# A two-layer graph network: ScalarE's one-hots ahead of its weight copies, and ranks summed right behind a group's last count

## The chip, the cores and the metric

The kernel runs on one core of a Trainium2 chip. The time is device microseconds of one execution. Three runs of the kernel before gave 1287.24, 1288.93 and 1292.48 us; the median is 1288.93.

## The reference

50,000 nodes with 256 features `x`, 12,500 edges with `src`, `dst` and 128 edge features. Two layers, each added to its input and normalised over the row (mean, variance):

```python
# layer 0: attention over incoming edges
h = x @ Wn.T + bn
e = edge_attr @ We.T + be
a = leaky_relu(sum((h[src] + e) * attn, -1), 0.01)
a = exp(a - segment_max(a, dst)[dst])
a = a / (segment_sum(a, dst)[dst] + 1e-16)
x = layernorm(x + relu(segment_sum(h[src] * a, dst)))
# layer 1: mean over neighbours (edge_index = [src, dst])
mean = segment_sum(x[dst], src) / max(count(src), 1)
x = layernorm(x + x @ W1.T + b1 + mean @ W2.T + b2)
```

Most nodes have no edge; for them layer 0 is only a normalisation.

## The kernel before, in words

The kernel is written for five engines by hand; each has its own program, and semaphores order them. Nothing is scheduled by a planner: the order on an engine is the order of its code.

**Tiles and groups.** The edges are 98 tiles of 128, padded to T = 100 tiles; four tiles are a group (Q = 25 groups). The nodes are 98 groups of 512 rows.

**Sorting by counting.** Edges are sorted twice, by `dst` (`DST`) and then by `src` (`SRC`). A key has a low digit (256 values) and a high digit (196). For every edge a one-hot row of each digit is made in `X`: VectorE (DVE, `onehots`) makes all low ones and five of eight high ones, ScalarE (ACT, `high_onehots`) the other three of eight, each in two steps (|digit - i| into a spare tile, then Relu(1 - it)). TensorE (PE, `sort`) multiplies them, eight matmuls a group, into a histogram in bank 7 that counts the edges of every key. DVE (`starts`) turns it into start positions, which PE seeds into the table in bank 2. Then come the *lookups* (DVE `tiles`, PE in `sort`, ACT): two tiles at a time ACT copies the table, PE adds the two tiles' counts to it, and looks up the copy with one-hots of the low digit spread across partitions (`low_across` on DVE, `upper_across` on ACT, made from low digits that SP loads). DVE compares keys within a tile (`earlier`), picks the looked-up count with `found_rank` two tiles later, and for a group sums both into ranks (`ranks`). During the DST lookups it also computes a product with the edge features (`features`).

**What the ranks release.** GpSimd (POOL) scatters one tile at a time of (key, other key, feature product) to its rank in HBM (`scatter_order`, line 506), each scatter waiting for the ranks of its group; at most 8 are in flight. When all 100 DST scatters have landed, `load_order` brings the sorted rows back (`ordrow`). DVE takes them in `ordered_rows(DST)` ahead of group 1 of the SRC lookups, and makes indices in `ordered_columns` and `ordered_ends` ahead of groups 2 and 3. With these, POOL gathers 100 tiles of `x` rows into `X` (line 497), then issues 20 SRC scatters, then 100 scatter-adds of layer 0's results into the copy `z_scratch` (line 544).

**Behind that.** DVE computes a dot of each gathered row with `v_b` (100 products), the softmax over the sorted edges follows, then layer 0's sums on PE. Then all node groups pass (`dense`, PE bound by its code), then the edges sorted by `src` (`by_src`).

**SP's queue.** In this order SP issues the key and weight loads, four loads of edge features, the low digits and keys spread over partitions for four groups (lines 396 and 398), then part of the 125 copies of `x` to `z_scratch` (line 372, 400 KB each): 20, two for every second group of DVE's DST one-hots, and then one or two for each group, with the spreads of later groups (three ahead) and more features between them. A second burst of copies is released by DVE's SRC one-hots. All copies must have landed before POOL's first scatter-add.

**The weights.** PE transposes Wn, W1 and W2 into banks 0 to 2 and forms products with the attention vector in banks 3 to 5. ACT copies them out: three copies of 128x512 (line 651) and three shorter ones (653 to 655), counted by `s_wcp`. PE waits for `s_wcp` = 4 ahead of `sort(DST)`, because the sort uses banks 1 to 6; DVE waits for it behind its DST one-hots, since `features` needs `u_b`. There DVE also adds the identity to W1 (line 1212), so that the residual comes with the product. `centre_weights` (behind the SRC lookups) takes the mean out of W1's and W2's columns.

Of the kernel before, what the change touches and what calls it, by code (L numbers as in the profile page):

```python
# [5 lines left out]
P = 128  # L6
D = 256
DE = 128
# [8 lines left out]
ALU = mybir.AluOpType  # L17
# [6 lines left out]
DST, SRC = 0, 1  # L24
ORDER_AT = 1
FLIGHT = 8
HOOK = 48


def wait(eng, sem, value):  # L30
# [23 lines left out]
def build(nc, x, src, dst, edge_attr, Wn, bn, We, be, attn, W1, b1, W2, b2, out):  # L54
# [24 lines left out]
    with ExitStack() as ctx:  # L79
# [10 lines left out]
        bank = [ctx.enter_context(nc.psum_tensor(f"bank{i}", [P, 512], F32)) for i in range(8)]  # L90
# [9 lines left out]
        w1T = sb("w1T", [P, 2, D])  # L100
# [507 lines left out]
        def _(act):  # L608
# [37 lines left out]
                act.wait_ge(s_keyf, 2 * k + 2)  # L646
                act.dma_start(lowrow_dram[k], lowrow[k]).then_inc(s_keyd[k], 16)

            for w, t in enumerate((wnT, w1T, w2T)):
                act.wait_ge(s_wt, w + 1)  # L650
                a.copy(t[:].rearrange("p b c -> p (b c)"), bank[w][:, :]).then_inc(s_wcp, 1)
            act.wait_ge(s_vu, 1)
            a.copy(v_b, bank[3][:, 0:D])
            a.copy(u_b[:], bank[4][:, 0:DE])
            a.copy(c0[:], bank[5][:, 0:1]).then_inc(s_wcp, 1)

            gaps = [0]

# [10 lines left out]
            def high_onehots(k, q):  # L669
                n = k * Q + q  # L670
                wait(act, s_hotA, n - 1)
                at = [(GT * q + j, gap_hi[2 * (n % 2) + j // 2]) for j in range(GT) if high_by_act(GT * q + j)]
                made = [gap(o, iota16[:, 0:HC], -1.0, dig_f[k][:, 1, t:t + 1]) for t, o in at]
                for (t, o), m in zip(at, made):
                    ins = is_zero(onehot_hi[:, t, :], o, m)
                ins.then_inc(s_hotA, 1)
# [19 lines left out]
            for k in (DST, SRC):  # L696
                if k == SRC:
                    act.wait_ge(s_add[DST], T)
                for q in range(Q):
                    high_onehots(k, q)  # L700
                act.wait_ge(s_hotA, (k + 1) * Q)
                if k == DST:
                    act.wait_ge(s_zero, 80)
                upper_across(k, 0)
                act.wait_ge(s_seed, k + 1)
                for i in range(T // 2):
                    wait(act, s_add[k], 2 * i)
                    wait(act, s_look[k], 2 * (i - 1))
                    a.copy(table[i % 2].rearrange("p b c -> p (b c)"), bank[2][:, 0:2 * HC]).then_inc(s_tab, 1)  # L709
                    if i % 2 == 0 and i // 2 + 1 < Q:  # L710
                        upper_across(k, i // 2 + 1)
                    if k == SRC and i == 2 * ORDER_AT + 5:
                        store_sorted(DST)
# [86 lines left out]
        def _(dve):  # L800
# [54 lines left out]
            def features(t):  # L855
                if t > FT:
                    return
                c, i = (t // EC, t % EC) if t < NEC * EC else (NEC + t - NEC * EC, 0)
                if i == 0:
                    dve.wait_ge(s_ea[c % 4], 16 * (c // 4 + 1))  # L860
                feature_dot(xin[c % 4], i, t, P if t < FT else LT)
# [39 lines left out]
            def ranks(k, q):  # L901
                dve.wait_ge(s_found[k], GT * q + GT)
                s = slice(GT * q, GT * q + GT)
                v.tensor_tensor(rank_i[k][:, s], earlier[:, s], found[:, s], ALU.add).then_inc(s_rank, 1)

            def tiles(k, between):
                low_across(k, 0)
                for q in range(Q):
                    n = k * Q + q
                    if q in between:  # L910
                        between[q]()
                    dve.wait_ge(s_kb[n % 4], 16 * (n // 4 + 1))
                    keys = keyB[n % 4]
                    for j in range(GT):
                        t = q * GT + j
                        odd = j % 2
                        if 2 <= t < GT:
                            dve.wait_ge(s_lbT, n + 2)
                        else:
                            wait(dve, s_found[k], t - 3)  # L920
                        ins = stt(pair_junk[odd], keys[:, (j - odd) * P:(j + 1) * P], pay[:, t:t + 1, k],
                                  earlier_mask[:, 1 - odd:2, :].rearrange("p b c -> p (b c)"), ALU.is_equal, ALU.mult,
                                  accum_out=earlier[:, t:t + 1])
                        if j == GT - 1:
                            ins.then_inc(s_kbu, 1)
                        if t >= 2:
                            found_rank(k, t - 2)
                        if k == DST:
                            features(t)
                        if j == 1 and q + 1 < Q:  # L930
                            low_across(k, q + 1)
                    if q >= 1:
                        ranks(k, q - 1)
                found_rank(k, T - 2)
                found_rank(k, T - 1)
                ranks(k, Q - 1)
# [115 lines left out]

            def centre_weights():

                pair_stats(0, P, 0, w1T[:])
                pair_stats(0, P, 1, w2T[:])
                then(v.tensor_tensor(bias_rows[:, 0, :], bias_rows[:, 0, :], bias_rows[:, 1, :], ALU.add))
                then(pair_stats(1, P, 0, bias_rows[:, 0:2, :]))
                for i, w in enumerate((w1T, w2T)):
                    for b in range(2):  # L1060
                        ins = ts(w[:, b, :], w[:, b, :], stats[:, 0, 2 * i + b, 1:2], None, ALU.subtract)
                then(ts(bias_rows[:, 0, :], bias_rows[:, 0, :], stats[:, 1, 0, 1:2], None, ALU.subtract))
                ins = v.tensor_copy(bias_rows[:, 1, :], bias_rows[:, 0, :])
                ins.then_inc(s_wcen, 1)
# [142 lines left out]

            then(v.memset(pay[:, FT:T, 2], 0.0))
            onehots(DST)
            dve.wait_ge(s_wcp, 3)  # L1210
            for b in range(2):
                v.tensor_tensor(w1T[:, b, b * P:(b + 1) * P], w1T[:, b, b * P:(b + 1) * P], ident[:], ALU.add)
            dve.wait_ge(s_wcp, 4)
            starts(DST)
            tiles(DST, {})
# [119 lines left out]
        def _(pe):  # L1335
# [47 lines left out]
            def sort(k, after):  # L1383
                hist, tab = bank[7][:, 0:2 * HC], bank[2][:, 0:2 * HC]
                pe.wait_ge(s_onehot, k * Q + 1)
                nothing(hist, start=True, stop=False)
                for t in range(T):
                    if t % GT == 0:
                        pe.wait_ge(s_onehot, k * Q + t // GT + 1)
                        pe.wait_ge(s_hotA, k * Q + t // GT + 1)  # L1390
                    count_tile(hist, t)
                nothing(hist, start=False, stop=True).then_inc(s_hist, 1)

                pe.wait_ge(s_rowtot, k + 1)
                tot = scanned[:, :, HC - 1:HC].rearrange("p b c -> p (b c)")
                mm(bank[1][:, 0:2], above[:], tot, start=True, stop=False, skip_group_check=True)
                mm(bank[1][:, 1:2], ones[:], tot[:, 0:1], start=False, stop=True, skip_group_check=True).then_inc(s_offs, 1)
                pe.wait_ge(s_base, k + 1)
                mm(tab, ident[:], base.rearrange("p b c -> p (b c)"), start=True, stop=False,
                   skip_group_check=True).then_inc(s_seed, 1)  # L1400

                for q in range(Q):
                    n = k * Q + q
                    for i in range(GT * q // 2, GT * q // 2 + GT // 2):
                        pe.wait_ge(s_tab, k * T // 2 + i + 1)
                        for t in (2 * i, 2 * i + 1):
                            count_tile(tab, t).then_inc(s_add[k], 1)
                        if 2 * i == GT * q:
                            pe.wait_ge(s_lbT, n + 1)
                            pe.wait_ge(s_lbA, n + 1)  # L1410
                        for t in (2 * i, 2 * i + 1):
                            wait(pe, s_found[k], t - 3)
                            j = t % GT
                            for b in range(2):
                                ins = mm(bank[3 + t % 4][:, 0:HC], onehotT[n % 2][:, b, j * P:(j + 1) * P], table[i % 2][:, b, :],  # L1415
                                         start=b == 0, stop=b == 1)
                            ins.then_inc(s_look[k], 1)
                    if q in after:
                        after[q]()
                nothing(tab, start=False, stop=True)  # L1420
# [35 lines left out]
                wait(pe, s_y, GT * (h - 2) + 2 * p + 2)  # L1456
                products(rbank(par, p), [(turned_rows(xT[2 * par + p], parts(h)), w1T)], parts(h)).then_inc(s_r, 1)

            pe.wait_ge(s_wcp, 4)
            sort(DST, {})  # L1460
            sort(SRC, {ORDER_AT: lambda: turn_ordered(DST), ORDER_AT + 1: lambda: shift_ordered(DST)})

# [153 lines left out]
```

## Time and profile before

| | |
|---|---|
| median of three runs | 1288.93 us (1287.24 to 1292.48) |
| profiled execution, its own time | 1285.87 us |
| its span, first to last instruction | 1284.1 us |
| mean granted TensorE clock | 0.935 |
| busy: PE, DVE, ACT, POOL | 1069.7, 970.6, 646.1, 752.2 us |
| HBM traffic | 236 GB/s over the span |

The profile is of one execution. A row of the timeline gives the start and the length in us, the engine, the line of the code, the operation and its tiles as output<-input, how many were merged into the row (x162), and in brackets the time for which the engine had nothing to do before it, with what ended that time. PEld is the loading of matmul weights, SPq, ACTq and POOLq are DMA issues. Tile names are given without their numbers; `own_rows`, `xT`, `sel`, `csel`, `agg` and `yout` are buffers with many uses. A row with [x us <-DMA y] says that the engine waited for a transfer into or out of y. A row that begins with a stretch (66.00:100.00) gives its length, the busy time and the instructions of PE, PEld, DVE, ACT and POOL in it, the granted clock, the busy share of the 16 DMA engines and GB/s. A row of the waits gives the total, the number and the longest. The granted clock is in parts of 2.4 GHz; 0.50 is the lower level, 1.2 GHz.

The stages, from the timeline: loads and weights to 22 us, DST one-hots to 52, DST lookups to 161, SRC one-hots to 193, SRC lookups to 303, dots and softmax to 372, layer 0's sums to 575, the pass over all nodes to about 1040, the edges by `src` to the end.

### The profile page before, as it was taken

What the parts mean: (1) busy time and instruction counts of PE and PEld (TensorE: products, weight loads), DVE (VectorE), ACT (ScalarE), POOL (GpSimd) and SP (SyncE); (2) the same over time, 40 slices, a digit from 0 to 9 for tenths busy, and PEclk for the clock granted to TensorE, in tenths of its full rate; (3) what the DMA queues carried; (4) which work ended last, traced back from release to release, by engine and by line L of the source; (5) the groups of instructions that cost most, each with busy time, mean ns of one, the idle gap of its engine ahead of it and who ended that gap; (6) DMA issues with size and microseconds to landing.
All of it is one profiled execution on the core that took longest, in us unless ns stands there. A gap on an engine that the chain in (4) does not pass through costs nothing. (4 is left out here: it accounts for less than half of the span.)

```text
span 1284.1 us, 23311 instructions
## 1 busy us (share of the span) xinstructions
PE 1069.7 (83%) x6258; PEld 942.2 (73%) x6258; DVE 970.6 (76%) x3610; ACT 646.1 (50%) x1525; POOL 752.2 (59%) x731
## 2 busy tenths in 40 slices
PE   4788867995069888409999999899999899999992
PEld 3577756884069777308888888788888699999882
DVE  8699996889765433318999999999999877776650
ACT  4756583561024332206776776577776544444441
POOL 1077772777778888854444410366565457777773
PEclk9899998998579999759999999999999999999997
DMA  5999795887627777655776776699999533333321
GB/s 162 330 258 268 179 254 139 270 256 271 250 53 121 106 104 103 71 113 198 244 245 239 244 245 242 222 327 317 328 329 326 181 99 122 114 127 120 121 87 48
DMA packets 118884, 251.51 MB, mean 196 GB/s; under 512 B 23908, under 2 KB 63959, under 8 KB 118802
## 3 DMA queue, kind: packets, MB, share of 16 engines
q1 hardware_dynamic: 75738, 183.99, 44.3%
q0 software_dynamic: 40432, 64.66, 22.4%
q10 hardware_dynamic: 2632, 1.89, 0.5%
q8 instruction: 37, 0.61, 0.2%
q14 instruction: 45, 0.37, 0.1%
HBM read 172.88 MB, written 130.62 MB: 236 GB/s over the span
## 5 line engine op out<-in xcount | busy, mean ns | idle before, releaser
L1436 PE MATMUL bank<-w1T,xT 128*128 128x256 f32 x1972 | 462.5, 381 | 2.1 <-ACT yout L624 2.0
L1436 PEld LDWEIGHTS bank<-w1T,xT 128*128 128x128 f32 x1972 | 365.7, 190 | 51.7 <-ACT xT L615 2.6
L506 POOL DMA_INDIRECT order_scratch<-pay,rank_i x200 | 195.4, 977 | 201.2 <-DVE xin L811 91.0
L624 ACT ACTIVATE yout<-bank,rstd 128x256 f32<-128x256 f32 x493 | 207.6, 488 | 21.9 <-DVE rstd L1330 21.4
L1047 DVE BATCH_NORM_STATS2 stats<-xin 128x6 f32<-128x512 f32 x239 | 154.0, 685 | 57.9 <-DMA xin<-z_scratch 27.7
L1047 DVE BATCH_NORM_STATS2 stats<-bank 128x6 f32<-128x512 f32 x247 | 166.2, 682 | 41.5 <-PE bank L1436 41.5
L544 POOL DMA_INDIRECT z_scratch<-xin,idx_out x100 | 156.1, 1561 | 32.6 <-issue 29.3
L619 ACT ACTIVATE std<-stats,eps_c 128x4 f32<-128x4 f32 x273 | 80.3, 301 | 183.1 <-DVE stats L1047 182.9
L497 POOL DMA_INDIRECT X<-z_scratch,idx_dst x100 | 95.5, 955 | 129.0 <-DVE xin L811 89.6
L811 DVE TENSOR_SCALAR xin<-xin,low_mean,rstd 128x256 f32<-128x256 f32 x477 | 167.0, 413 | 0.9
L1415 PE MATMUL bank<-sel,agg 128*128 128x196 f32 x800 | 158.8, 342 | 4.5 <-DVE bank L814 4.5
L1427 PE MATMUL bank<-ident,xin 128*128 128x128 f32 (+1 forms) x952 | 127.8, 274 | 34.8 <-DVE xin L811 34.7
L615 ACT COPY xT<-bank 128x512 f32<-128x512 f32 x247 | 145.6, 590 | 15.6 <-PE bank L1427 9.8
L1427 PEld LDWEIGHTS bank<-ident,xin 128*128 128x128 f32 (+1 forms) x952 | 112.0, 142 | 46.4 <-issue 34.6
L1415 PEld LDWEIGHTS bank<-sel,agg 128*128 128x128 f32 x800 | 134.5, 196 | 6.9 <-DVE bank L814 6.2
L500 POOL DMA_INDIRECT out_rows<-yout,idx_out x100 | 100.0, 1000 | 62.8 <-issue 52.4
L1501 PE MATMUL bank<-sel,X 128*128 128x128 f32 x800 | 109.2, 288 | 23.0 <-ACT agg L723 20.6
L1501 PEld LDWEIGHTS bank<-sel,X 128*128 128x128 f32 x800 | 104.2, 202 | 29.4 <-ACT agg L723 21.6
L497 POOL DMA_INDIRECT X<-in_x,idx_src x100 | 99.0, 990 | 44.5 <-issue 18.0
L1366 PE MATMUL bank<-X 128*128 128x196 bf16 x800 | 96.2, 257 | 32.7 <-ACT sel L709 17.0
L814 DVE SCALAR_TENSOR_TENSOR xin<-bank,xdot,own_rows 128x256 f32<-128x256 f32 x100 | 42.1, 477 | 95.7 <-DMA z_scratch<-xin,idx_out 78.9
L1366 PEld LDWEIGHTS bank<-X 128*128 128x128 bf16 x800 | 67.4, 101 | 61.8 <-ACT sel L709 31.8
(250 smaller groups left out, 1405.5 us busy)
## 6 DMA issues: line engine op xcount, KB each, us to landing
z_scratch<-in_x SPq DMA_DIRECT2D x125, 400.0 KB
xin<-z_scratch SPq DMA_DIRECT2D x97, 512.0 KB, 4.6
out_rows<-yout SPq DMA_DIRECT2D x97, 512.0 KB, 3.0
kB<-sorted_scratch SPq DMA_DIRECT2D x50, 256.0 KB, 3.4
yout<-keys_scratch SPq DMA_DIRECT2D x50, 128.0 KB
xin<-in_edge_attr SPq DMA_DIRECT2D x12, 512.0 KB, 7.5
yout<-low_digits_scratch SPq DMA_DIRECT2D x50, 64.0 KB
order_scratch<-pay,rank_i POOLq DMA_INDIRECT x200
```

Source lines behind the costliest of these rows:

```text
L497: g.indirect_dma_start(out=dst_ap, out_offset=None, in_=table, in_offset=where).then_inc(s, 16)
L506: g.indirect_dma_start(out=order_dram[k], out_offset=bass.IndirectOffsetOnAxis(ap=rank_i[k][:, t:t + 1], axis=0), in_=pay[:, t, :], in_off ...
L544: g.indirect_dma_start(out=z_dram, out_offset=column(idx_out[DST], GT * q + j), in_=xin[q % 4][:, j, :], in_offset=None, compute_op=ALU.ad ...
L615: a.copy(xT[dst_i][:].rearrange("p a b c -> p (a b c)"), src_bank[:, :]).then_inc(copied, 1)
L624: a.activation(yout[hu][0:rows, j, :], bank_of(j // 2)[0:rows, (j % 2) * D:(j % 2 + 1) * D], ACT.Copy, scale=rstd[0:rows, slot, j:j + 1]). ...
L811: return v.tensor_scalar(o, i, s1, s2, o0, o1) if o1 is not None else v.tensor_scalar(o, i, s1, s2, o0)
L1047: return v.bn_stats(stats[0:rows, slot, 2 * p:2 * p + 2, :].rearrange("p j s -> p (j s)"), pair.rearrange("p j c -> p c j"))
L1366: ins = mm(o[:, b * HC:(b + 1) * HC], onehot_lo[:, t, b * P:(b + 1) * P], onehot_hi[:, t, :], start=False, stop=False, skip_group_check=True)
L1415: ins = mm(bank[3 + t % 4][:, 0:HC], onehotT[n % 2][:, b, j * P:(j + 1) * P], table[i % 2][:, b, :], start=b == 0, stop=b == 1)
L1427: ins = tr(o[:, at:at + n], pair[0:n, jj, c * P:(c + 1) * P], ident[0:n, 0:n])
L1436: ins = mm(to, left, w, start=i == 0, stop=i == len(pieces) - 1)
L1501: ins = mm(bank[b][:, j * P:(j + 1) * P], X[:, GT * q + j, c * P:(c + 1) * P], sel[q % 2][:, j, :], start=True, stop=True)
```

## The change

It has four edits:

1. On ACT the weight copies move into a function that is called ahead of group 10 (`WEIGHTS_AT`) of the DST high one-hots; ten groups of one-hots now come first.
2. PE's wait for the weight copies moves from ahead of the DST histogram to behind it, ahead of the first matmul that writes bank 1.
3. DVE adds the identity to W1 in `centre_weights`, with a wait for the result, instead of between its DST one-hots and the start positions.
4. In the lookups DVE sums the ranks of group q-1 behind the second tile of group q, right after the last count of group q-1, instead of behind the fourth. This holds for both sorts.

```diff
+WEIGHTS_AT = 10
...
-            for w, t in enumerate((wnT, w1T, w2T)):
-                act.wait_ge(s_wt, w + 1)
-                a.copy(t[:].rearrange("p b c -> p (b c)"), bank[w][:, :]).then_inc(s_wcp, 1)
-            act.wait_ge(s_vu, 1)
-            a.copy(v_b, bank[3][:, 0:D])
-            a.copy(u_b[:], bank[4][:, 0:DE])
-            a.copy(c0[:], bank[5][:, 0:1]).then_inc(s_wcp, 1)
+            def copy_weights():
+                for w, t in enumerate((wnT, w1T, w2T)):
+                    act.wait_ge(s_wt, w + 1)
+                    a.copy(t[:].rearrange("p b c -> p (b c)"), bank[w][:, :]).then_inc(s_wcp, 1)
+                act.wait_ge(s_vu, 1)
+                a.copy(v_b, bank[3][:, 0:D])
+                a.copy(u_b[:], bank[4][:, 0:DE])
+                a.copy(c0[:], bank[5][:, 0:1]).then_inc(s_wcp, 1)
...
                 for q in range(Q):
+                    if k == DST and q == WEIGHTS_AT:
+                        copy_weights()
                     high_onehots(k, q)
...
                         if k == DST:
                             features(t)
+                        if j == 1 and q >= 1:
+                            ranks(k, q - 1)
                         if j == 1 and q + 1 < Q:
                             low_across(k, q + 1)
-                    if q >= 1:
-                        ranks(k, q - 1)
...
             def centre_weights():
 
+                for b in range(2):
+                    ins = v.tensor_tensor(w1T[:, b, b * P:(b + 1) * P], w1T[:, b, b * P:(b + 1) * P], ident[:], ALU.add)
+                then(ins)
                 pair_stats(0, P, 0, w1T[:])
...
             onehots(DST)
-            dve.wait_ge(s_wcp, 3)
-            for b in range(2):
-                v.tensor_tensor(w1T[:, b, b * P:(b + 1) * P], w1T[:, b, b * P:(b + 1) * P], ident[:], ALU.add)
             dve.wait_ge(s_wcp, 4)
             starts(DST)
...
                 pe.wait_ge(s_rowtot, k + 1)
+                pe.wait_ge(s_wcp, 4)
...
-            pe.wait_ge(s_wcp, 4)
             sort(DST, {})
```

On ACT, behind the last DMA of the key rows, this stood before (own_rows<-iota is the first step of a one-hot, X<-own_rows the second):

```order
L651 ACT_TABLE_LOAD
L651 COPY own_rows<-bank 128x512
L651 COPY w1T<-bank 128x512
L651 COPY w2T<-bank 128x512
L653 COPY own_rows<-bank 128x256
L654 COPY u_b<-bank 128x128
L655 COPY c<-bank 128x1
L662 ACTIVATE own_rows<-iota,own_rows 128x196 x2
L667 ACTIVATE X<-own_rows,ones 128x196 x2
```

Now the table load is followed by ten groups of one-hots, of which the ninth and tenth stand here, and only then by the copies:

```order
L664 ACTIVATE own_rows<-iota,own_rows 128x196 x2
L669 ACTIVATE X<-own_rows,ones 128x196 x2
L664 ACTIVATE own_rows<-iota,own_rows 128x196
L669 ACTIVATE X<-own_rows,ones 128x196
L653 COPY own_rows<-bank 128x512
L653 COPY w1T<-bank 128x512
L653 COPY w2T<-bank 128x512
L655 COPY own_rows<-bank 128x256
L656 COPY u_b<-bank 128x128
L657 COPY c<-bank 128x1
```

The copies moved behind the tenth group; nothing on ACT was added or dropped.

On DVE, in group 1 of the DST lookups (bank,found is `found_rank`, xin,pay is `features`, xT,earlier the comparison within a tile, agg<-yout is `low_across` for the next group), this stood before, from the second tile's count to the end of the group:

```order
L814 SCALAR_TENSOR_TENSOR bank6,found<-own_rows2,own_rows5,bank6 128x196
L814 SCALAR_TENSOR_TENSOR xin0,pay<-xin0,u_b 128x128
L811 TENSOR_SCALAR agg0<-yout2,slot_f 128x512
L814 SCALAR_TENSOR_TENSOR xT0,earlier<-yout1,pay,own_rows2 128x128
L814 SCALAR_TENSOR_TENSOR bank3,found<-own_rows2,own_rows5,bank3 128x196
L814 SCALAR_TENSOR_TENSOR xin0,pay<-xin0,u_b 128x128
L814 SCALAR_TENSOR_TENSOR xT0,earlier<-yout1,pay,own_rows2 128x256
L814 SCALAR_TENSOR_TENSOR bank4,found<-own_rows2,own_rows5,bank4 128x196
L814 SCALAR_TENSOR_TENSOR xin0,pay<-xin0,u_b 128x128
L904 TENSOR_TENSOR rank_i0<-earlier,found 128x4
```

and this stands now:

```order
L818 SCALAR_TENSOR_TENSOR bank6,found<-own_rows2,own_rows5,bank6 128x196
L818 SCALAR_TENSOR_TENSOR xin0,pay<-xin0,u_b 128x128
L908 TENSOR_TENSOR rank_i0<-earlier,found 128x4
L815 TENSOR_SCALAR agg0<-yout2,slot_f 128x512
L818 SCALAR_TENSOR_TENSOR xT0,earlier<-yout1,pay,own_rows2 128x128
L818 SCALAR_TENSOR_TENSOR bank3,found<-own_rows2,own_rows5,bank3 128x196
```

The ranks moved ahead of the low one-hot and of two tiles' work. One feature product lies between the count into bank 6, the last that these ranks need, and the ranks.

## Rows read from the trace of the kernel before

**Rows 1.** Page, part 1: busy us, share of the span, instructions.
```profile
PE 1069.7 (83%) x6258; PEld 942.2 (73%) x6258; DVE 970.6 (76%) x3610; ACT 646.1 (50%) x1525; POOL 752.2 (59%) x731
```

**Rows 2.** Timeline from 11 to 52 us: ACT, DVE and PE at the one-hots.
```profile
11.27 1.28 ACT L651 ACT_TABLE_LOAD   x1 [11.27 <-issue]
...
12.32 30.82 DVE L811 TENSOR_SCALAR X<-iota,own_rows 128x256 bf16<-128x256 bf16 x162
...
19.68 0.59 ACT L651 COPY w2T<-bank 128x512 f32<-128x512 f32 x1 [0.27 <-PE bank L1348]
...
22.20 0.83 ACT L662 ACTIVATE own_rows<-iota,own_rows 128x196 bf16<-128x196 bf16 x2
...
23.86 6.14 PE L1366 MATMUL bank<-X 128*128 128x196 bf16 x48 [1.14 <-ACT X L667]
...
49.73 0.79 ACT L667 ACTIVATE X<-own_rows,ones 128x196 bf16<-128x196 bf16 x2
...
51.77 1.01 DVE L876 TENSOR_TENSOR_SCAN csel<-own_rows,bank 128x196 f32<-128x196 bf16 x2 [8.22 <-PE bank L1362]
```

**Rows 3.** Timeline from 63 to 66 us: the first ranks.
```profile
63.38 0.48 DVE L811 TENSOR_SCALAR agg<-yout,slot_f 128x512 f32<-128x512 uint8 x1
...
65.56 0.16 DVE L904 TENSOR_TENSOR rank_i<-earlier,found 128x4 int32<-128x4 f32 x1
...
66.02 1.16 POOL L506 DMA_INDIRECT order_scratch<-pay,rank_i  x1 [60.31 <-DVE rank_i L904]
```

**Rows 4.** Timeline from 195 to 220 us: the last DST scatter to the first gather.
```profile
195.27 0.96 POOL L506 DMA_INDIRECT order_scratch<-pay,rank_i  x1 [0.30 <-issue]
...
204.93 0.62 POOL L517 DMA_DIRECT2D ordrow<-order_scratch  x1 [8.70 <-DMA order_scratch<-pay,rank_i]
...
207.70 0.24 DVE L940 COPY krow<-ordrow 100x128 f32<-100x128 f32 x1 [6.56 <-DMA ordrow<-order_scratch]
...
219.86 1.02 POOL L497 DMA_INDIRECT X<-in_x,idx_src  x1 [14.31 <-DVE idx_out L967]
```

**Rows 5.** Last gather, first scatter-add; waits of 200 to 380 us; one stretch.
```profile
348.15 0.95 POOL L497 DMA_INDIRECT X<-in_x,idx_src  x1 [0.30 <-issue]
...
377.44 1.64 POOL L544 DMA_INDIRECT z_scratch<-xin,idx_out  x1 [2.47 <-ACT xin L734]
...
DVE xT L814 <- DMA X<-in_x,idx_src: 6.7, 9, 0.9
...
340.00:360.00 20.00, 1.78 (x9) 0.91 (x9) 10.68 (x51) 0.00 (x0) 15.12 (x17) 0.50 0.20 56
```

**Rows 6.** SP's queue, waits for its loads, and the stretch of the DST lookups.
```profile
30.84 17.51 SPq L372 DMA_DIRECT2D z_scratch<-in_x  x26
...
54.85 0.33 SPq L396 DMA_DIRECT2D yout<-low_digits_scratch  x1
...
96.19 0.72 ACT L662 ACTIVATE own_rows<-yout,slot_f 128x512 bf16<-128x512 uint8 x1 [2.13 <-DMA yout<-low_digits_scratch]
...
99.33 0.43 DVE L814 SCALAR_TENSOR_TENSOR bank<-own_rows,bank 128x196 f32<-128x196 f32 x1 [0.33 <-PE bank L1415]
...
66.00:100.00 34.00, 28.83 (x198) 25.83 (x197) 33.67 (x213) 18.42 (x32) 25.28 (x26) 1.00 1.03 268
```

**Rows 7.** PE's lookups around DVE's wait, and the granted clock in that stretch.
```profile
208.97 2.98 PE L1415 MATMUL bank<-sel,agg 128*128 128x196 f32 x8 [3.82 <-DVE bank L814]
...
215.48 1.52 PE L1415 MATMUL bank<-sel,agg 128*128 128x196 f32 x8
...
208.00:214.00 6.00, 5.03 (x18) 4.88 (x19) 5.09 (x32) 1.82 (x3) 0.00 (x0) 0.50 0.21 47
```

**Rows 8.** Timeline: two dependent DVE steps; DVE in the SRC lookups.
```profile
218.14 0.26 DVE L960 TENSOR_TENSOR xdot<-keyc,prevk 128x100 f32<-128x100 f32 x1
218.44 0.26 DVE L961 TENSOR_TENSOR idx_tmp<-idx_tmp,xdot 128x100 f32<-128x100 f32 x1
...
298.43 0.43 DVE L814 SCALAR_TENSOR_TENSOR bank<-own_rows,bank 128x196 f32<-128x196 f32 x1 [0.58 <-PE bank L1415]
```

## The prediction

> **What bounds the kernel now.** I read the page first, then the timeline from the start, then POOL's own timeline. GpSimd (POOL) is busy for 59% of the span [rows 1], yet from 66 to 575 us it is the engine that the others follow: 100 order scatters, 100 gathers, 20 scatters, 100 scatter-adds, nearly without a pause. So the question is when POOL may start, and what holds it between its blocks.
>
> Its start hangs on the first histogram. VectorE (DVE) makes its one-hots from 12.32 to 43.14, while ScalarE (ACT) loads its table at 11.27, waits for the weight transposes, copies the weights and begins its one-hots at 22.20; its last ends at 50.52, and DVE gets the histogram at 51.77 after 8.22 us without work [rows 2]. The first ranks are written at 65.56 and POOL starts at 66.02, after 60.31 us of idling [rows 3].
>
> Next, POOL's first block ends: the last DST scatter is issued at 195.27, POOL waits 8.70 us for it to land, loads the order rows at 204.93, and DVE, which had reached that point of the SRC lookups, takes them at 207.70 after waiting 6.56 us. From them come the indices with which the gathers start at 219.86, POOL having idled 14.31 us [rows 4]. DVE reached the wait at 207.70 - 6.56 = 201.14. These two arrivals, POOL's chain and DVE's, decide the gain.
>
> What follows is released by that work. The last gather is issued at 348.15; DVE's last dots wait for gathers, 6.7 us in 9 waits; the scatter-adds begin at 377.44 [rows 5]. A shift of 219.86 should reach the end whole. The background copy of x, which must be done before 377.44, has DMA engines only 0.20 busy from 340 to 360 [rows 5], so it has about 17 us to spare.
>
> **The change, part by part.**
>
> *ACT's one-hots first.* Table load ends at 11.27 + 1.28 = 12.55, and digits and iota exist by then (DVE's start at 12.32 uses them). ACT's 25 groups took 50.52 - 22.20 = 28.32 us, 1.133 a group [rows 2]. Ten groups end at 12.55 + 11.33 = 23.9. The six copies: three are 0.59 us each [rows 2] and three shorter, so between 1.8 and 3.5 us; I take 2.3, nearer the low end because the short ones are half the size or less. ACT resumes at 26.2 and its last 15 groups end at 43.2, level with DVE's 43.14. With the lag seen before (50.52 to 51.77, 1.25 us) DVE gets the histogram at 44.4 instead of 51.77: **7.3 us earlier** (between 6.1 and 7.4 by the copies). TensorE (PE) must keep up: 200 counting matmuls at the 128 ns of its first batch, 48 in 6.14 us [rows 2], would take 25.6 us; from 22.2 that ends at 47.8 and leaves 4.0 us. But that batch worked off a backlog; I take the one-hots as the end and keep 4.0 as the low bound.
>
> *Ranks two tiles earlier.* In the DST lookups the sum moves from 65.56 to where DVE now starts the next low one-hot, 63.38: **2.2 us earlier** [rows 3]. POOL needs no other thing at that moment, so it starts 7.3 + 2.2 = 9.5 us earlier, at 56.5. Its pace, (195.27 - 66.02) / 99 = 1.31 us a scatter, 5.2 a group, is its own; ranks come faster than that. The last scatter is issued at 185.8, lands at 195.4 with the same wait, and the order rows are with DVE at 198.2.
>
> *What of the 7.3 us DVE's lookups keep.* Little, by this trace. SP queues 26 copies of 400 KB from 30.84 on for 17.51 us, released by one-hots that DVE makes at the same times as before. The loads of low digits and keys for the lookups stand behind them on the same queue, the first issued at 54.85, and from 66 to 100 the DMA engines are fully busy. At group 10 ACT still waits 2.13 us for its low digits (96.19), and DVE, through PE, 0.33 us (99.33) [rows 6]. So at that point the lookups have no lead over the loads. Starting them earlier does not start the copies earlier; these loads land when the copies and feature loads ahead of them are through. Bounds: nothing kept (DVE at 201.1 again) and all kept (193.8). I take 0.5, by the row at 99.33, which is the point of the stage that binds.
>
> That sets the order rows (198.2) before DVE (200.6): DVE no longer waits, and it is DVE's own arrival that ends last. Gain: 207.70 - 200.6 = 7.1 us. Late next is PE: while DVE waited, PE had run two lookup pairs ahead, which now lie on the path (its pair takes 1.52 us at the full clock, 215.48). Against this, PE idled 3.82 us before 208.97 and then had its granted clock at 0.50 (the level of 1.2 GHz) from 208 to 214, with 2.98 us for such a pair; without that idle time it should stay at the upper level and save 1.5 us there and 1 us in the next [rows 7]. I set the two against each other: zero, with 1 us either way.
>
> *Small edits.* The identity is added to w1T in the node-weight centring instead of in the 8.22 us gap: two 128x128 adds, under 1 us with a wait, covered by DVE's 6.7 us of waiting for gathers [rows 5]; without that cover up to 1 us. PE's wait for the weight copies moves behind the histogram, when they are 15 us old: nothing. In the SRC lookups the ranks now follow their last count directly. A waited DVE step there costs little: of two dependent steps, 0.26 us long, the second starts 0.30 us after the first, and DVE idles 0.58 us a group waiting for PE [rows 8]. In the DST lookups, where DVE has no idle time, a feature product (two DVE steps) lies between count and ranks, longer than the 0.04 us that the waiting step loses in that row. Both nothing; without product and idle time the row would give 24 x 0.04 = 1.0 us on DVE's arrival, and a sum of 6.1.
>
> The Trainium skill (VectorE: DVE Perf Modes, "The DRAIN you can't avoid") says that a semaphore between two DVE operations costs nothing extra, as the pipeline is emptied between them in any case. By that rule even the bare wait would be free and the sum would stay at 7.1; the 0.04 us in rows 8 are nearly that.
>
> **Sum.** 7.1 us. The profiled execution took 1285.87 us and would take 1278.8; it is 3.1 us below the median, 1288.93, from which I forecast **1281.8 us**. Some 0.5% (6.4 us) is what a measurement here tells from no change, so the forecast is just past it.
>
> **Rivals.**
> - *The lookups keep all 7.3 us* (loads overtake, or the queue had slack). DVE is at its wait at 193.8, the order rows come at 198.2 and decide: 9.5 us, 1279.4. For it: DVE is at work for 33.67 of the 34 us from 66 to 100 [rows 6], so the stage looks like DVE's. Against: the wait at group 10. Chance 0.20.
> - *The last scatter lands early as well.* POOL's landing wait of 8.70 us [rows 4] would have to be its neighbours' doing, and gone. If it fell by 4 us, the order rows came at 194.2, and with all of the shift kept the gain would be 13.5 us, 1275.4. The Trainium skill (DMA: Bandwidth & Descriptors, "Queues, rings and completion order") says that each DMA engine takes turns between the queues that have work, by which POOL's few bytes would not wait behind SP's copies. The 8.70 us were measured with such copies in flight, so the trace does not bear it out. Chance 0.03.
> - *The landing does not move.* The second burst of SP's copies runs beside the last scatters; if their landing goes by the end of that burst, which moves only with DVE, the order rows come at 203 to 206 and the gain is 2 to 5 us, say 1285.4. Against it stands only that the wait begins with POOL's own last issue. Chance 0.15.
> - *Slower: the moved ranks stall DVE in the DST lookups.* DVE has no idle time there [rows 6]. If the new wait cost 0.4 us in each of 24 groups, DVE would reach its wait at 201.1 + 9.6 = 210.7, 3 us later than now: 1291.9. It decides from (207.70 - 201.14) / 24 = 0.27 us a group. The row of 0.30 us between dependent steps speaks against it, and the feature product in between. Chance 0.05.
> - *The forecast*, DVE's arrival sets the gain, 5.5 to 8 us: 0.57. That ACT does start early is plain from its order; that the histogram then waits for PE instead is inside it, since 4.0 + 2.2 = 6.2 us on POOL's chain still gives 6.2.
>
> **How the numbers follow.** Faster by over 0.5%: the two early cases (0.23) and some three fifths of the forecast, whose lower part lies inside 0.5%: 0.57. Slower by over 0.5%: 0.04, the stall with its upper price. The rest, 0.39, within 0.5%. The range runs from 9.5 us of gain with 2 us for the scatter of medians (the runs shown span 5 us) to a gain of 3.5 with the same: 1277.4 to 1287.4.
>
> **What will show it.** After: ACT's first one-hot at 12.6; DVE's idle time before the scan from 8.22 to about 1 us; POOL's first scatter at 56 to 57; ACT waits for low digits in groups four to ten longer than before (the queue takes the shift back) and DVE's SRC one-hots starting at nearly the old time; no wait before the order rows; gathers starting 7 us earlier, and the same 7 us at 377 and at the end. The prediction is wrong if DVE's SRC one-hots start 4 us or more earlier (then more is gained), or if the order rows still make DVE wait with its arrival unmoved (then less).

## The result, and the profile after

The change made the kernel slower. Over 20 runs of each on one chip the changed kernel took 1294.68 us (1289.37 to 1297.25) and the kernel before 1289.33 us (1285.85 to 1294.62): ratio 1.0036, 95% interval 1.0025 to 1.0048, or 5.35 us more. The forecast was 1281.8 us with a range up to 1287.4: wrong in sign, and the median lies outside. The profiled execution has a span of 1291.9 us, against 1284.1 us before; single executions differ by a few us, so stages are compared between the two traces, and times between medians.

The timeline of the changed kernel, all engines, in order of time (start, duration, engine, line, what, and in brackets the idle time before it and what ended it):

```profile
13.15 0.81 ACT L664 ACTIVATE own_rows<-iota,own_rows 128x196 bf16<-128x196 bf16 x2
...
31.91 18.26 SPq L373 DMA_DIRECT2D z_scratch<-in_x  x26
44.95 1.01 DVE L880 TENSOR_TENSOR_SCAN csel<-own_rows,bank 128x196 f32<-128x196 bf16 x2 [1.18 <-PE bank L1366]
50.27 0.94 SPq L397 DMA_DIRECT2D yout<-low_digits_scratch  x1
55.28 0.15 DVE L908 TENSOR_TENSOR rank_i<-earlier,found 128x4 int32<-128x4 f32 x1
55.74 1.16 POOL L507 DMA_INDIRECT order_scratch<-pay,rank_i  x1 [50.03 <-DVE rank_i L908]
59.15 12.99 SPq L373 DMA_DIRECT2D z_scratch<-in_x  x2
63.38 0.15 DVE L908 TENSOR_TENSOR rank_i<-earlier,found 128x4 int32<-128x4 f32 x1
71.93 0.96 POOL L507 DMA_INDIRECT order_scratch<-pay,rank_i  x1 [0.66 <-issue]
76.09 0.72 ACT L664 ACTIVATE own_rows<-yout,slot_f 128x512 bf16<-128x512 uint8 x1 [14.82 <-DMA yout<-low_digits_scratch]
76.09 0.49 DVE L815 TENSOR_SCALAR agg<-yout,slot_f 128x512 f32<-128x512 uint8 x1 [12.56 <-DMA yout<-low_digits_scratch]
82.09 0.16 DVE L908 TENSOR_TENSOR rank_i<-earlier,found 128x4 int32<-128x4 f32 x1
82.53 0.96 POOL L507 DMA_INDIRECT order_scratch<-pay,rank_i  x1 [9.64 <-DVE rank_i L908]
...
198.90 1.05 POOL L507 DMA_INDIRECT order_scratch<-pay,rank_i  x1 [0.30 <-issue]
210.86 0.62 POOL L518 DMA_DIRECT2D ordrow<-order_scratch  x1 [10.92 <-PE bank L1370]
216.62 0.24 DVE L944 COPY krow<-ordrow 100x128 f32<-100x128 f32 x1 [6.32 <-DMA ordrow<-order_scratch]
228.65 1.02 POOL L498 DMA_INDIRECT X<-in_x,idx_src  x1 [17.18 <-DVE idx_out L971]
387.06 1.63 POOL L545 DMA_INDIRECT z_scratch<-xin,idx_out  x1 [2.33 <-ACT xin L738]
```

Up to 55.74 all went as meant. ACT's one-hots start at 13.15, the histogram is with DVE at 44.95 (51.77 in [rows 2]), the first ranks at 55.28 and POOL's first scatter at 55.74 (65.56 and 66.02 in [rows 3]): 10.3 us earlier. Then comes a wait that the kernel before did not have: until 76.09 DVE (from 63.5) and ACT (from 61.3) stand still for the low digits of group 4, whose load SP had issued at 50.27, 4.6 us *earlier* than before [rows 6]. POOL, which had scattered the ranks of three groups, runs out of ranks for 9.64 us. Its last scatter is issued at 198.90, 3.6 us later than in [rows 4], and the first gather at 228.65, 8.8 us later. (Ahead of the order rows `load_order` waits for nothing but the landing of the scatters; where the brackets name PE there, here and below, the profile guessed wrongly.)

What the DMA engines did in that time is seen in the stretches (busy us and count by engine, then granted clock, DMA share, GB/s). First the kernel before, then the changed one:

```profile
core 0: us, PE busy (x) PEld busy (x) DVE busy (x) ACT busy (x) POOL busy (x), PEclk, DMA share, GB/s
56.00:62.00 6.00, 5.42 (x24) 5.02 (x24) 2.77 (x16) 2.69 (x5) 0.00 (x0) 0.56 1.00 311
62.00:66.00 4.00, 3.70 (x26) 3.33 (x26) 4.00 (x27) 2.30 (x4) 0.00 (x0) 1.00 0.95 312
66.00:70.00 4.00, 3.70 (x27) 3.30 (x26) 4.00 (x25) 2.30 (x4) 3.07 (x3) 1.00 0.67 222
```

```profile
56.00:62.00 6.00, 5.40 (x38) 4.89 (x38) 6.00 (x41) 3.11 (x6) 4.78 (x5) 1.00 1.04 326
62.00:66.00 4.00, 1.79 (x13) 1.49 (x11) 1.53 (x11) 0.00 (x0) 3.09 (x4) 1.00 1.11 131
66.00:70.00 4.00, 0.00 (x0) 0.00 (x0) 0.00 (x0) 0.00 (x0) 2.15 (x3) 0.56 0.92 227
70.00:76.00 6.00, 0.00 (x0) 0.00 (x0) 0.00 (x0) 0.00 (x0) 1.93 (x3) 0.50 1.10 185
```

In the kernel before, the engines moved some 310 GB/s until 66 us and POOL had nothing in flight. In the changed kernel POOL issues scatters from 55.74 on. Their first packets show on the DMA engines between 60 and 62 us, when the rate is still 354 GB/s; from 62 to 66 the engines, busy throughout, move 131 GB/s. PE falls idle as well, and its granted clock drops to 0.50, the level of 1.2 GHz.

### The profile page after: what moved, and what is told of

Read it like the earlier page. It is cut to its first block and busy times, and to the rows that moved or that the text cites. A ratio compares the mean times of both kernels' runs of the same rounds, so it can differ in the third digit from the quotient of the medians.

```text
span 1291.9 us, 23312 instructions
## 1 busy us (share of the span) xinstructions
PE 1063.7 (82%) x6258; PEld 942.7 (73%) x6258; DVE 973.2 (75%) x3610; ACT 645.0 (50%) x1525; POOL 757.6 (59%) x731
## 5 line engine op out<-in xcount | busy, mean ns | idle before, releaser
L507 POOL DMA_INDIRECT order_scratch<-pay,rank_i x200 | 199.1, 995 | 200.6 <-DVE xin L815 90.5
L1370 PE MATMUL bank<-X 128*128 128x196 bf16 x800 | 92.4, 252 | 45.6 <-ACT sel L713 33.0
```

The lines of the kernel that those rows point to most:

```text
L507: g.indirect_dma_start(out=order_dram[k], out_offset=bass.IndirectOffsetOnAxis(ap=rank_i[k][:, t:t + 1], axis=0), in_=pay[:, t, :], in_off ...
L1370: ins = mm(o[:, b * HC:(b + 1) * HC], onehot_lo[:, t, b * P:(b + 1) * P], onehot_hi[:, t, :], start=False, stop=False, skip_group_check=True)
```

## The experiments

**Theory T**: the order scatters (POOL's), now earlier, run beside SP's burst of 26 copies and slow it, so that the loads behind the burst land late. **Rival O**: queue order alone; the load stands behind the copies and lands when it lands, and earlier lookups only wait longer. **Rival M**: the moved ranks hold up DVE or PE. **Rival C** (later): the placing of SP's copies is all that matters. All runs were timed in five rounds against the kernel before on the same chip; that kernel's median was 1286.76 us in the first four, 1286.85 in the next four, 1285.81 in the last. Expectations were written on the base of 1289; ratios are what can be compared.

**1. The scatters held back until group 4's low digits are there.** `s_lb[0]` reaches 32 with the second load into the first buffer, that of group 4.

```diff
+            pool.wait_ge(s_lb[0], 32)
             for t in range(T):
                 pool.wait_ge(s_rank, t // GT + 1)
```

> The changed kernel, with one wait more: POOL issues no order scatter of DST until the low digits of group 4 have landed. Theory T (scatters slow the burst): the copies on SP's queue lose their rate only because POOL's 12-byte scatters, now issued from 55.7 us, run beside them. With the scatters held back the burst drains at some 310 to 330 GB/s as in the kernel before, the low digits of group 4 land at about 66 to 69 us, and DVE's wait before group 4 falls from 12.6 to some 3 to 5 us; the lookups then end 7 to 9 us earlier than in the changed kernel, and the time is 1284 to 1288 us, if POOL catches up by the end of the lookups. Rival O (queue order alone: the load stands behind the copies and lands when it lands): the wait stays near 12 us and the time at 1294. Rival M (the moved ranks hold up DVE or PE): nothing changes, 1294 us.

Measured: 1293.9 us, ratio 1.0056 (1.0043 to 1.0069). The timeline:

```profile
31.37 17.14 SPq L373 DMA_DIRECT2D z_scratch<-in_x  x26
...
69.93 0.48 DVE L816 TENSOR_SCALAR agg<-yout,slot_f 128x512 f32<-128x512 uint8 x1 [6.96 <-DMA yout<-low_digits_scratch]
70.20 1.24 POOL L507 DMA_INDIRECT order_scratch<-pay,rank_i  x1 [64.48 <-DMA yout<-low_digits_scratch]
75.92 0.16 DVE L909 TENSOR_TENSOR rank_i<-earlier,found 128x4 int32<-128x4 f32 x1
193.10 1.01 DVE L881 TENSOR_TENSOR_SCAN csel<-own_rows,bank 128x196 f32<-128x196 bf16 x2 [1.11 <-PE bank L1367]
202.40 0.96 POOL L507 DMA_INDIRECT order_scratch<-pay,rank_i  x1 [0.30 <-issue]
```

And the DMA view of both kernels from 62 to 66 us (queue q1 carries SP's copies and loads, q0 POOL's scatters; packets, MB, time as a share of 16 engines). Changed kernel:

```profile
DMA packets 173, 0.52 MB, mean 131 GB/s; under 512 B 71, under 2 KB 71, under 8 KB 173
q1 hardware_dynamic: 123, 0.52, 108.6%
q0 software_dynamic: 50, 0.00, 2.3%
```

Scatters held back:

```profile
DMA packets 315, 1.24 MB, mean 311 GB/s; under 512 B 52, under 2 KB 75, under 8 KB 315
q1 hardware_dynamic: 315, 1.24, 100.8%
```

The stretch and the order of the queue are the same and only the scatters are gone: 311 GB/s instead of 131. A packet of SP's queue took on average 4 us x 16 x 1.008 / 315 = 0.20 us without scatters, and 4 x 16 x 1.086 / 123 = 0.57 us with them (a sum above 100% means that packets overlap), while the 50 packets of the scatters took 2.3% themselves. This is the worst stretch, not a constant: from 62 us until the load is there the means are 182 GB/s with scatters (to 76) and 277 without (to 70), and run 2 below, with scatters but a shorter burst, moves 335 GB/s from 62 to 66. DVE's wait fell from 12.56 to 6.96 us (T had expected 3 to 5) and the load was there at 69.93 instead of 76.09 (0.5 us of that because the burst began earlier). So both T and O hold a part: about 5.6 us of the wait is the scatters' doing and 7.0 us plain queue order. DVE's SRC scan is back at 193.10, where the kernel before had it (193.21). That the time did not fall, against T's figure, is POOL's: it did not catch up. It issued a scatter every (202.40 - 70.20) / 99 = 1.34 us and issued the last at 202.40, 7.1 us after the kernel before [rows 4].

**2. Ten copies less ahead of group 4**

```diff
             for i in range(10):
                 sp.wait_ge(s_onehot, 2 * i + 1)
-                copy_x(2)
+                copy_x(1)
```

> The changed kernel, with one copy of x instead of two at each of the ten steps of SP's early burst (16 copies instead of 26 ahead of the loads of group 4; the ten left over go out at the end of the sort with the others). Theory T and rival O both say that the loads of group 4 then stand behind 10 copies less, worth about 10 x 400 KB at 320 GB/s = 12.5 us: they land by about 57 us, before the lookups of group 4 need them (63.5 us), and the wait of 12.6 us goes. What is left of the 6.8 us by which the first lookups start earlier is kept: some 1278 to 1283 us, unless the ten copies cost their time again beside the gathers. Rival M (moved ranks): the stall stays and so does 1294 us.

Measured: 1281.44 us, ratio 0.9951 (0.9938 to 0.9964), 5.3 us faster than the kernel before. DVE no longer waits at group 4, and with ranks at their moved place: rival M, as written for DVE and PE, is out. Where it gains and what it gives back:

```profile
190.98 0.96 POOL L507 DMA_INDIRECT order_scratch<-pay,rank_i  x1 [0.30 <-issue]
195.36 0.62 POOL L518 DMA_DIRECT2D ordrow<-order_scratch  x1 [3.42 <-PE bank L1370]
210.99 1.02 POOL L498 DMA_INDIRECT X<-in_x,idx_src  x1 [15.01 <-DVE idx_out L971]
293.01 31.86 SPq L373 DMA_DIRECT2D z_scratch<-in_x  x33
373.67 1.64 POOL L545 DMA_INDIRECT z_scratch<-xin,idx_out  x1 [5.40 <-ACT xin L738]
```

The first gather is 8.9 us earlier than in [rows 4], the first scatter-add only 3.8 us earlier than in [rows 5]. 33 copies instead of 23 now go out beside the gathers, and POOL waits 5.40 us instead of 2.47 for ACT's rows before the first scatter-add. Run 5 below shows that the one causes the other: it is the kernel before with only these ten copies moved there, and it waits 6.13 us, with 161.1 instead of 157.6 us from first gather to first scatter-add. Run 7, with 23 copies there, waits 2.48.

**3. and 4. Each part alone.** Run 3 is the changed kernel with `ranks(k, q - 1)` put back behind the group's last tile; run 4 the kernel before with only the ranks moved.

> The changed kernel with the ranks put back to where they were, after the group's last tile. First ranks some 2.2 us later than in the changed kernel, so POOL's first scatter at about 58 instead of 55.7 us. Theory T: the scatters still start well inside the burst, the stall before group 4 is shorter by at most 2 or 3 us: 1291 to 1294 us. Rival M (the moved ranks are to blame): the stall goes, 1280 to 1283 us. Rival O: as the changed kernel, 1294.

> The kernel before with the ranks alone moved ahead of the group's last two tiles; ScalarE's one-hots stay behind the weight copies. POOL's first scatter at about 63.8 instead of 66.0 us, when the burst (over at about 66 to 68 us) is nearly drained. Theory T: a loss of 0 to 3 us against a gain of up to 2 us at the end of the DST lookups: 1287 to 1291 us. Rival M: slower by most of the 5 us that the change cost, 1293 to 1295 us. Rival O: no change or 2 us faster.

Measured: one-hots alone 1289.15 us, ratio 1.0016 (1.0000 to 1.0032), with 9.5 us of waiting at group 4; ranks alone 1288.41 us, ratio 1.0012 (1.0002 to 1.0022), with no such wait on DVE. Neither part is worth anything in this queue, and together they cost more than either (1.0036). The stall fits T: POOL starts at 65.25 (ranks alone, in a trace whose histogram came 2.9 us later than in [rows 2]), 59.02 (one-hots alone) or 55.74 us (both), the earlier, the more of the burst its scatters meet, and DVE waits at group 4 not at all, 9.52 and 12.56 us. M wanted the stall gone in run 3. T's figure of 2 to 5 us lost there was just about met, with 2. The times of runs 3 and 4 are not T's alone, though: the moved ranks have a price of their own on POOL, which is read behind run 8.

**5. to 8. Room in the queue.** Run 5 is the kernel before with the edit of run 2, its control. Run 6 takes the burst out of the changed kernel altogether. Run 7 moves ten copies of it ahead of SP's wait for the weights, so that they fill a time when the kernel before moved 5 GB/s (16 to 20 us) and 34 (20 to 24); it moves 394 and 345 there:

```diff
+            copy_x(10)
             sp.wait_ge(s_wt, 3)
             sp.wait_ge(s_vu, 1)
...
             for i in range(10):
                 sp.wait_ge(s_onehot, 2 * i + 1)
-                copy_x(2)
+                copy_x(1)
```

Run 8 is run 2 with the ranks at their old place.

> The kernel before with SP's early burst cut from 26 to 16 copies as in the run with ten copies less: the control for that run. Theory T: in the kernel before nothing waited for these loads, so nothing is gained in the DST lookups; the ten copies that go out later, beside the gathers of x, may cost up to the 5 us that the stretch from first gather to first scatter-add grew by there (157.6 us before, 162.7 with ten copies less): 1287 to 1292 us. Rival C (the shorter burst by itself made that run fast, whatever ScalarE does): 1281 to 1283 us.

> The changed kernel with the burst taken out: 6 copies instead of 26 ahead of the loads of group 4, 20 more at the end of the sort. Theory T: with 16 copies nothing waited any more at group 4, so the DST lookups gain at most 1 or 2 us more; the stretch of the gathers takes the second ten copies as well and grows by up to another 5 us: 1281 to 1287 us. If copies beside the gathers cost nothing: 1279 to 1281 us.

> The changed kernel with ten copies issued right behind the weight loads, where the queues moved 5 GB/s from 16 to 20 us and 34 from 20 to 24 us, and ten instead of twenty in the burst: 26 copies ahead of group 4 as in the changed kernel, and as many at the end. Theory T: the burst is drained some 8 to 10 us earlier, the low digits of group 4 land at about 60 to 64 us, DVE's wait there falls from 12.6 to 0 to 2 us, the first gather starts at 211 to 213 us and the gathers keep their 158 us: 1277 to 1281 us. Rival (the early copies hold up the keys, the low digits or the features that the first lookups need): the DVE scan is late by several us and the time is 1284 to 1290 us.

> The run with ten copies less, with the ranks put back to where they were before. Theory T: once the queue is clear, POOL's 100 scatters of DST at 1.31 us each start when the first ranks are there, so ranks 2.2 us later make the last landing, the order rows and the gathers 2 us later: 1282 to 1284 us against 1280 to 1282. Rival M (the moved ranks cost time on DVE): faster than that run, 1278 to 1280 us. If neither: the same.

| run | median us | ratio to before (95%) |
|---|---|---|
| 5: before, ten copies less | 1287.86 | 1.0010 (0.9997 to 1.0022) |
| 6: changed, burst out | 1280.44 | 0.9949 (0.9933 to 0.9965) |
| 7: changed, ten copies at the start | 1279.07 | 0.9937 (0.9919 to 0.9955) |
| 8: run 2 with old ranks | 1280.47 | 0.9952 (0.9936 to 0.9969) |

Run 5: the shorter burst alone gains nothing in the end (2.0 us at the first gather, given back by the ten copies beside the gathers), so C is out. Run 6 is no better than run 2: once nothing waits at group 4, still less in the queue is worth nothing. Run 7 is the fastest. Its timeline:

```profile
7.95 6.92 SPq L370 DMA_DIRECT2D z_scratch<-in_x  x10
35.33 10.10 SPq L370 DMA_DIRECT2D z_scratch<-in_x  x16
...
55.75 1.16 POOL L508 DMA_INDIRECT order_scratch<-pay,rank_i  x1 [50.03 <-DVE rank_i L909]
189.71 0.96 POOL L508 DMA_INDIRECT order_scratch<-pay,rank_i  x1 [0.30 <-DMA order_scratch<-pay,rank_i]
194.28 0.62 POOL L519 DMA_DIRECT2D ordrow<-order_scratch  x1 [3.61 <-PE bank L1371]
210.19 1.02 POOL L499 DMA_INDIRECT X<-in_x,idx_src  x1 [15.29 <-DVE idx_out L972]
369.47 1.63 POOL L546 DMA_INDIRECT z_scratch<-xin,idx_out  x1 [2.48 <-ACT xin L739]
```

POOL starts at the same moment as in the changed kernel (55.75), with as many copies ahead of group 4, and nothing waits there; the first gather is 9.7 us earlier than in [rows 4] and the first scatter-add 8.0 us earlier than in [rows 5]. The time is 7.8 us below that kernel's. Run 8 was the run on the ranks alone: T expected some 2 us slower than run 2, M faster, and it came out the same (0.9952 against 0.9951). Its order rows are loaded at 197.04, 1.7 us later than in run 2, but that does not show in the time.

Runs 2 and 8 differ in the ranks' place alone, and POOL tells them apart. In run 8 it starts 1.2 us later (58.49 against 57.31) and yet issues its last scatter 2.6 us *earlier* (188.37 against 190.98). A scatter itself takes POOL longer where the ranks are moved. All 100 DST scatters of five kernels (count: shortest, median and longest in ns, first and last start), in the order before, run 8, run 4, run 2, changed:

```profile
L506 POOL DMA_INDIRECT order_scratch<-pay,rank_i x100: 954/959/1218, 66.0 to 195.3; - x100
L507 POOL DMA_INDIRECT order_scratch<-pay,rank_i x100: 954/959/1162, 58.5 to 188.4; - x100
L506 POOL DMA_INDIRECT order_scratch<-pay,rank_i x100: 955/1008/1202, 65.2 to 198.9; - x100
L507 POOL DMA_INDIRECT order_scratch<-pay,rank_i x100: 955/1010/1200, 57.3 to 191.0; - x100
L507 POOL DMA_INDIRECT order_scratch<-pay,rank_i x100: 954/1012/1201, 55.7 to 198.9; - x100
```

The first two have the old ranks, the others the moved ones. So it is in all eleven traces: the median is 958 or 959 ns in the five kernels with old ranks and 1008 to 1024 in the six with moved ones, and the 100 scatters take 98.3 to 98.9 us in all against 102.7 to 103.8. Where nothing stalls, POOL issues one every 1.31 us with old and every 1.35 us with moved ranks. Some 4 us on POOL's block is more than the 2.2 us of earlier start that the move was to bring. Why a scatter takes longer then, no run tells.

**9. The control for run 7**: the kernel before with the edit of run 7.

> The kernel before with the same placing of copies as the fastest run so far: ten behind the weight loads, ten instead of twenty in the burst. The control for that run. Theory T: in the kernel before no engine waited for the loads behind the burst, so clearing them earlier is worth at most a microsecond or two: 1285 to 1288 us. Rival C (the placing of the copies alone makes the gain of 8 us, whatever ScalarE does): 1279 to 1281 us.

Measured: 1283.72 us, ratio 0.9988 (0.9975 to 1.0002); its first gather is at 218.83, 1.0 us earlier than in [rows 4]. So of the 0.63% of run 7 the placing of the copies by itself gives 0.12%, with an interval that holds zero; the rest needs the change as well. The early one-hots and the cleared queue are worth something only together.

## Why the prediction was wrong

**ACT's one-hots first: right.** Predicted: one-hots from 12.6, ACT back from the weight copies at 26.2, histogram at 44.4. Measured: 13.15, 26.23, 44.95.

**Ranks two tiles earlier, first part: right.** First scatter predicted at 56.5, measured at 55.74.

**"Its pace ... is its own; ranks come faster than that": the step that failed.** It moved POOL's whole block by its first scatter. In the changed kernel POOL waits 9.64 us for ranks at its thirteenth scatter, and its block takes 143.16 us instead of 129.25. Three things were wrong with the step, and only the last two needed the chip to be seen.
- It sits badly with the next step. If the lookups keep only 0.5 of the 7.3 us, and lose the rest as early as group 4, as they did, ranks from the fourth group on come nearly at their old times, and POOL, 10 us ahead, must run dry. (Lost only by group 10, where the prediction looked, it need not have: POOL takes 5.2 us for a group, and DVE makes the ranks of one in 4.13.) In run 1 the fourth ranks come at 75.92, against 77.94 in the kernel before. The thirteenth scatter could then start at about 76.4, against 81.98 before: an estimate of 5.6 us left of 9.5, even if the scatters harmed nobody. The chain over POOL would have ended last, not DVE's arrival, and the forecast should have been 1.5 us higher (5.6 us of gain for 7.1).
- Nothing in the sum priced what the scatters do to the transfers that they now meet. I had asked for the copies' effect on the scatters (two rivals on the landing) but not for the reverse. The wait at group 4 became 12.56 us, 5.6 us of it from the scatters by run 1, and POOL's thirteenth scatter came at 82.53: the whole lead was gone, and 0.6 us more.
- The pace is not POOL's own either: with the moved ranks the 100 scatters take 102.7 us of POOL's time instead of 98.9, which would have used up 3.8 of those 5.6 us.

**"These loads land when the copies and feature loads ahead of them are through": right as a mechanism, short by the scatters' part.** Without scatters (run 1) DVE's SRC scan comes 0.1 us earlier than before; predicted 0.5. With them it comes at 201.32, 8.1 us later. It goes on from there: the second burst of copies is released by DVE's SRC one-hots, so it starts at 170.18 instead of 162.10 and is drained at about 204 instead of 199, in both after POOL's last issue.

The difference at the first gather, 228.65 - 219.86 = 8.79 us, adds up along POOL's chain: the start -10.28, its block of 100 scatters 143.16 instead of 129.25 us (+13.91, of which 9.64 is the wait at the thirteenth and 3.8 the longer scatters), last scatter to load of the order rows 11.96 instead of 9.66 (+2.30), load to first gather 17.79 instead of 14.93 (+2.86, all of it the load itself: 5.76 us until DVE has the rows, against 2.77). Behind that the stretch to the first scatter-add grew by 0.83 us and the rest shrank by 1.82: 7.8 us of span.

**PE's clock and run-ahead: not tried.** DVE still waits for the order rows in the changed kernel (6.32 us) and in run 7, so the case on which that term rested did not come about.

**Small edits at nothing: right for DVE.** In run 7, where no load holds them up, the third and fourth ranks are 4.06 us apart (63.38 and 67.44), the first two of the kernel before 4.13 (65.56 and 69.69). The waiting rank step costs DVE nothing that shows. What the moved ranks do to POOL's scatters had no term in the sum.

**The rivals.** The slower one, by the moved ranks, had the right sign for a wrong reason: runs 2 and 7 have moved ranks and no stall. "The lookups keep all 7.3 us" (9.5 us) is what run 7 shows of the lookups when the queue is cleared: DVE is at its wait for the order rows at 192.29, 8.9 us earlier. That the first gather comes 9.7 us earlier, so near that rival's figure, is luck: POOL's block took 133.96 us (+4.7) and the wait for the landing, from last issue to load, 4.57 us instead of 9.66 (-5.1). "The last scatter lands early as well" had 0.03, and in runs 2 and 7 it does (4.38 and 4.57 us). "The landing does not move" was nearer than its chance of 0.15. It has the landing go by the end of SP's second burst, which moves only with DVE. In ten of the eleven kernels the order rows are loaded some 4 to 7 us after that burst has drained (after the last stretch of 1 us at its rate: about 199 before, 204 in the changed kernel, 191 in run 2, 192 in run 8, 190 in run 7), however late the last scatter was issued: run 8 issued it 2.6 us earlier than run 2 and had it landed 1.7 us later. In the changed kernel DVE came late, so the burst and the landing were later too. In run 1 the last scatter was issued at 202.40, after the burst, and POOL still waited 6.45 us. No run moved the second burst by itself, so this stays a reading of the traces. The Trainium skill (DMA: Bandwidth & Descriptors, "Queues, rings and completion order") has the DMA engines take turns between queues. That fits the 50 scatter packets that got through in the 4 us above; that each of the other queue's packets then takes nearly three times as long does not follow from it.

Why a packet of SP's queue takes longer beside scatters (their size, their addresses or their count in flight) stays open; no run here tells these apart.

## What to carry to other kernels

When a step that issues many small transfers is moved earlier, look at what is in flight at its new time, and price the harm in both directions, to it and by it. A consumer that starts earlier is worth only what its producer can keep up: carry the times of the producer's later items through, not the first one alone, and don't take the consumer's pace for a constant. And a background burst that nobody waits for in one version can become the longest wait in the next, so move it to a time when the queues are empty (here 0.6% faster than the kernel before, where the change without it was 0.4% slower).

## What the hardware showed that I had not expected

A busy DMA engine is not one that moves bytes. From 62 to 66 us the engines' share was 1.11 at 131 GB/s with scatters of 12 bytes a row beside the copies, and 1.01 at 311 GB/s without; the scatters' own packets took 2.3%. SP is held up as well: behind the burst two copies took it 12.99 us to issue at 59.15, and 9.49 us in run 1 without scatters, where in the kernel before two copies at 66.09, when the burst was through, took 1.40 us. And an engine's own step of the same size is not always equally long: POOL's scatter takes 0.96 or 1.01 us by where another engine's four-column sum stands.
